# Twelve looked-up tables instead of thirteen, 56 gathers instead of 52, and another place for the last transposes

## What is computed

```python
e = jnp.stack([tbl_0[ids[:, 0]], tbl_1[ids[:, 1]], ..., tbl_25[ids[:, 25]]], axis=1)
all_emb = jnp.concatenate([r_bottom_output[:, None, :], e], axis=1)
z = jnp.einsum('bfd,bgd->bfg', all_emb, all_emb)[:, _TRIU_I, _TRIU_J]
h = jnp.concatenate([z, r_bottom_output], axis=1)
h = jnp.maximum(h @ W_top1 + b_top1, 0.0)
h = jnp.maximum(h @ W_top2 + b_top2, 0.0)
y = h @ W_top3
```

## Time and profile before

| | us |
|---|---|
| median of three runs | 112.02 |
| the three runs | 111.33, 112.02, 112.22 |
| the profiled execution, whole | 113.11 |
| its span in the trace | 111.3 |
| PE busy | 102.7 (92%) |
| PEld busy | 87.2 (78%) |
| DVE busy | 67.5 (61%) |
| ACT busy | 62.0 (56%) |
| POOL busy | 55.9 (50%) |

### The profile page before, as it was taken

One profiled execution on the slowest core, in us unless ns is written; L12 is line 12 of the kernel. 1 busy time (PEld: TensorE's weight loads), 2 busy tenths in 40 slices (PEclk: granted clock), 3 DMA queues, 4 the chain that ended last, 5 costly groups with the idle time before them and its releaser, 6 DMA issues.

```text
span 111.3 us, 3670 instructions
## 1 busy us (share of the span) xinstructions
PE 102.7 (92%) x1562; PEld 87.2 (78%) x1562; DVE 67.5 (61%) x151; ACT 62.0 (56%) x105; POOL 55.9 (50%) x59
## 2 busy tenths in 40 slices
PE   4999999999999999899958999976999989999992
PEld 4767778887888887788947889865999978997970
DVE  3599999999999989999980006400910550082010
ACT  5535996992894899986573124242343246234331
POOL 2777787777777777777777777740000000000000
PEclk9999999999999999999999999999999999999999
DMA  2989999999999999999961212220000000000000
GB/s 73 286 243 233 198 236 211 235 228 221 204 223 236 208 229 231 229 198 226 239 175 47 53 53 53 68 56 0 6 6 0 6 6 0 6 9 0 0 0 0
DMA packets 6369, 13.72 MB, mean 123 GB/s; under 512 B 1984, under 2 KB 2640, under 8 KB 6354
## 3 DMA queue, kind: packets, MB, share of 16 engines
q1 hardware_dynamic: 4520, 10.02, 39.6%
q0 software_dynamic: 1664, 3.41, 13.5%
q10 hardware_dynamic: 170, 0.07, 0.3%
HBM read 13.48 MB, written 0.02 MB: 121 GB/s over the span
## 4 chain that ended last, share of the span: by engine, by line
PE 49%; POOL 24%; issue 12%; DMA 9%; ACT 3%; ACTq 0%
POOL rows L328 24%; PE acc L683 11%; PE acc L649 10%; DMA rows<-tbl,ids_sb 7%; PE ring L693 7%; PE acc L614 6%; PE acc L588 6%; PE acc L674 3%; PE ring L626 3%; PE ring L703 2%; DMA ids_sb<-ids 2%; PE ring L657 1%; ACT emb L400 1%; ACT onehot L389 1%; ACT away L384 0%
## 5 line engine op out<-in xcount | busy, mean ns | idle before, releaser
L328 POOL DMA_INDIRECT rows<-tbl,ids_sb x52 | 55.2, 1061 | 17.2 <-issue 15.5
L498 DVE TENSOR_SCALAR onehot<-far 125x512 fp32r<-125x512 f32 x102 | 38.2, 434 | 1.9 <-ACT far L359 1.9
L588 PE MATMUL acc<-onehot,hi 125*128 125x512 f32 x94 | 26.2, 404 | 0.2 <-DVE onehot L498 0.2
L588 PE MATMUL acc<-onehot,lo 125*128 125x512 f32 x94 | 25.0, 390 | 0.0
L508 DVE COPY gram<-acc 128x432 f32<-128x432 f32 x4 | 3.7, 922 | 29.8 <-PE acc L649 29.8
L588 PEld LDWEIGHTS acc<-onehot,lo 125*128 125x128 f32 x94 | 17.7, 188 | 3.8
L588 PEld LDWEIGHTS acc<-onehot,hi 125*128 125x128 f32 x94 | 16.7, 188 | 4.8 <-DVE onehot L498 1.7
L345 ACT CAST hi<-raw 125x1024 fp32r<-125x1024 f32 (+1 forms) x12 | 13.3, 1105 | 11.3 <-DMA raw<-tbl 6.8
L485 DVE TENSOR_TENSOR lo<-raw,hi 125x512 fp32r<-125x512 f32 (+1 forms) x26 | 18.4, 710 | 0.0
L649 PE MATMUL acc<-emb 128*27 128x27 f32 x1024 | 12.9, 192 | 2.7 <-issue 2.7
L649 PEld LDWEIGHTS acc<-emb 128*27 128x27 f32 x1024 | 10.9, 104 | 5.1 <-issue 3.5
(11 more groups left out here) (41 smaller groups left out, 77.9 us busy)
## 6 DMA issues: line engine op xcount, KB each, us to landing
raw<-tbl SPq DMA_DIRECT2D x9, 448.0 KB
raw<-tbl SPq DMA_DIRECT2D x3, 560.0 KB
ids_b<-ids SPq DMA_DIRECT2D x4, 256.0 KB, 10.6
rows<-tbl,ids_sb POOLq DMA_INDIRECT x52, 8.3
w1z<-w SPq DMA_DIRECT2D x1, 702.0 KB
w_sb<-w SPq DMA_DIRECT2D x1, 512.0 KB
raw<-tbl SPq DMA_DIRECT2D x9, 52.0 KB
raw<-tbl SPq DMA_DIRECT2D x2, 224.0 KB
```

The source lines that it names most:

```text
L328: nc.gpsimd.indirect_dma_start(out=rows[:, t, slot, :], out_offset=None, in_=tables[table], in_offset=bass.IndirectOffsetOnAxis(ap=ids_sb[ ...
L498: ins = nc.vector.tensor_scalar(onehot[:, n % OH_RING, k, :], far[:, t % FAR_RING, :], float(c), None, ALU.is_equal)
L588: mm = nc.tensor.matmul(acc[:, look_bank(t), :], part_of[:, t % HL_RING, c * D:(c + 1) * D], onehot[:, n % OH_RING, k, :], start=(half == ...
```

## The change

Table 13 is no longer looked up but gathered. That leaves 12 looked-up tables (table 12 moves behind table 18) and 14 gathered ones, in four groups a tile of 4, 4, 4 and 2. Pairs are now (0,1), (2,3), up to (10,11), and the last table's chunks are all compared by VectorE. Turn (2,0) no longer stands behind a look; the turns of tile 2 follow later in the second part of the order, and turns (3,2) and (3,3) stand ahead of `bottom` (2,1).

```diff
-LOOKED_UP = [1, 2, 4, 8, 16, 17, 12, 18, 20, 13, 21, 24, 25]
-LONG = [8, 12, 13]
+LOOKED_UP = [1, 2, 4, 8, 16, 17, 18, 12, 20, 21, 24, 25]
+LONG = [8, 12]
...
-    behind = {2: (0, 0), 3: (0, 1), 4: (0, 2), 5: (0, 3), 6: (1, 0), 7: (1, 1), 8: (1, 2), 9: (1, 3), 10: (2, 0)}
+    behind = {2: (0, 0), 3: (0, 1), 4: (0, 2), 5: (0, 3), 6: (1, 0), 7: (1, 1), 8: (1, 2), 9: (1, 3)}
...
-              ("turn", 2, 1),
+              ("turn", 2, 0),
...
-              ("gram", 0, 2), ("part", NL - 1, 2), ("turn", 2, 2), ("gram", 0, 3), ("part", NL - 1, 3),
-              ("turn", 2, 3), ("bottom", 0, 0), ("bottom", 0, 1), ("gram", 1, 0), ("turn", 3, 0), ("bottom", 1, 0),
+              ("gram", 0, 2), ("part", NL - 1, 2), ("turn", 2, 1), ("gram", 0, 3), ("part", NL - 1, 3),
+              ("bottom", 0, 0), ("bottom", 0, 1), ("turn", 2, 2), ("gram", 1, 0), ("bottom", 1, 0),
...
 def paired(j):
 
-    return j > 0 and (NL - 1 - j) % 2 == 0
+    return j % 2 == 1
 
 
 def by_act(j):
 
-    return LOOKED_UP[j] in LONG or paired(j)
+    return LOOKED_UP[j] in LONG or paired(j) and j < NL - 1
...
-        idb_in = [sem(f"idb_in{k}") for k in range((NL - FIRST + 1) // 2)]
+        idb_in = [sem(f"idb_in{k}") for k in range((NL - FIRST) // 2)]
...
-                    n = 2 if paired(t) else 1
-                    if paired(t) or t == 0:
-                        first, b = slot_of(t - n + 1), look_bank(t - n + 1)
+                    if paired(t):
+                        first, b = slot_of(t - 1), look_bank(t - 1)
...
-                        pe.wait_ge(emb_look, t - LOOK + (1 if paired(t - LOOK) or t == LOOK else 2))
+                        pe.wait_ge(emb_look, (t - LOOK) // 2 * 2 + 2)
```

More of the change, by code:

```diff
@@ L107, in work_order @@
     order += [("compare", NL - 1, 0), ("part", NL - 2, 0), ("part", NL - 2, 1), ("part", NL - 1, 0), ("part", NL - 1, 1),
-              ("turn", 2, 1),
+              ("turn", 2, 0),
               ("gram", 0, 0), ("part", NL - 2, 2), ("gram", 0, 1), ("part", NL - 2, 3),
-              ("gram", 0, 2), ("part", NL - 1, 2), ("turn", 2, 2), ("gram", 0, 3), ("part", NL - 1, 3),
-              ("turn", 2, 3), ("bottom", 0, 0), ("bottom", 0, 1), ("gram", 1, 0), ("turn", 3, 0), ("bottom", 1, 0),
[L112 to L116, removed]
+              ("gram", 0, 2), ("part", NL - 1, 2), ("turn", 2, 1), ("gram", 0, 3), ("part", NL - 1, 3),
+              ("bottom", 0, 0), ("bottom", 0, 1), ("turn", 2, 2), ("gram", 1, 0), ("bottom", 1, 0),
+              ("gram", 1, 1), ("pairs", 0, 0), ("turn", 2, 3), ("gram", 1, 2), ("l1", 0, 0), ("l1", 0, 1), ("gram", 1, 3),
+              ("l1", 0, 2), ("l1", 0, 3), ("turn", 3, 0), ("bottom", 1, 1),
+              ("gram", 2, 0), ("l2", 0, 0), ("gram", 2, 1), ("l2", 0, 1), ("pairs", 1, 0), ("bottom", 2, 0), ("turn", 3, 1),
+              ("gram", 2, 2), ("l1", 1, 0), ("l1", 1, 1), ("gram", 2, 3), ("l1", 1, 2), ("l1", 1, 3), ("turn", 3, 2),
+              ("turn", 3, 3), ("bottom", 2, 1),
               ("gram", 3, 0), ("l2", 1, 0), ("gram", 3, 1), ("pairs", 2, 0), ("l2", 1, 1), ("l3", 0, 0),
@@ L279, in load_ids @@
             def load_ids(k):
[L280 to L283, removed]
+                sp.dma_start(ids_b[:, 2 * k:2 * k + 2, :].rearrange("p j b -> p (j b)"),
+                             ids_16[FIRST + 2 * k:FIRST + 2 * k + 2, :].rearrange("j b -> (j b)").unsqueeze(0)
+                             .broadcast_to([128, 2 * B])).then_inc(idb_in[k], 16)
             sp.dma_start(idt_i[:], ids_t).then_inc(idt_in, 16)
@@ L395, in _ @@
                         split(t + HL_RING)
-                    n = 2 if paired(t) else 1
-                    if paired(t) or t == 0:
-                        first, b = slot_of(t - n + 1), look_bank(t - n + 1)
+                    if paired(t):
+                        first, b = slot_of(t - 1), look_bank(t - 1)
                         act.wait_ge(oh_used, 2 * (t + 1))
-                        nc.scalar.copy(emb[:, :, :, first:first + n],
-                                       acc[:, b:b + n, :].rearrange("d j (t p) -> d t p j", t=TILES)
-                                       ).then_inc(emb_look, n)
+                        nc.scalar.copy(emb[:, :, :, first:first + 2],
+                                       acc[:, b:b + 2, :].rearrange("d j (t p) -> d t p j", t=TILES)
+                                       ).then_inc(emb_look, 2)
                     if t == NL // 2:
```

## The result

| | before, us | changed, us | ratio, 95% interval |
|---|---|---|---|
| first series | 112.02 | 109.19 | 0.9723 (0.968 to 0.9767) |
| second series, another chip | 112.69 | 108.95 | 0.9697 (0.9637 to 0.9756) |

The forecast was 108.9, a ratio of 0.972, within 107.2 to 110.6. The kernel became about 3% faster. Times are medians of all executions, ratios go by the fast ones alone, and the profiled execution of the first series was a slow one (112.3 us, with TensorE's granted clock at 0.50 from 48.3 to 51.7), so the profile read here is that of the second series: 108.96 us, span 107.0, granted clock 1.0 in every slice. The trace of the kernel before was taken with the first series, so the two traces compared are of different series.

What follows compares the result with a forecast made beforehand. The looks were held by TensorE, VectorE, DMA engines and gather issue together, the second part by TensorE. Terms -4.0 (looks), +0.5 (transposes) and +0.4 (stops) sum to -3.1 us: 112.02 becomes 108.9, range 107.2 to 110.6.

Steps and rivals of the forecast that it cites:

- What bounds: Looks: TensorE, VectorE and DMA engines nearly equally full, with gathers at their own pace; from gram (0,0) on, TensorE.
- milestone 1: Start of turn (1,2) in the looks: gather 26 lands at 46.7, start at 46.8, 1.8 us later; TensorE idles about 2.
- Milestone 2: Turn (1,2) to first gram: onehot wait goes, last cast is late next; parts end at 55.5, 4.0 us earlier.
- The last turns: Turn (3,3) ahead of the bottom product: gains nothing beyond 0.11 to 0.2; tile 3's gram 1.7 us after turn (3,2).
- The second part: From gram (0,0) to the end, bound by TensorE: +0.5 us for transposes and +0.4 for stops.
- the transposes: Behind gram (0,0): 24 instead of 18, +0.66 with some given back, net +0.5 us (bounds 0.2 and 1.2).
- TensorE's stops: Inside grams, at boundaries 127 or 128 matmuls apart that shift by 21: +0.4 us (bounds -1.0 and +1.5).
- the gathers land in time: Rival at turn (1,2): gather 26 lands before 44.7, parts end 1.4 to 2.0 earlier, time 107.3 us; chance 0.15.
- The worse join: Rival at the last table's parts: late gather 32, cast or compares, parts take 5.8 us, time 111.0; chance 0.12.
- Late last gathers: Rival at turn (3,3): gather 56 lands late, at 88.8 taking back 2.8 us, at 91.8 giving 114.7; chance 0.04.

Runs made afterwards that it cites:

- f1_act_last: Changed kernel with the last table's chunk 0 made by ScalarE again, on a third chip: 110.75 us, ratio 0.9826.
- c2_turn_late: Changed kernel with turn (1,2) one look later, behind look 9, and turn (1,3) behind the parts: 107.97 us, ratio 0.9607.
- a4_act_last: Changed kernel with the last table's chunk 0 made by ScalarE again, on a slow chip: 158.75 us against 162.03 for the kernel before.
- e1_act_last: Changed kernel with the last table's chunk 0 made by ScalarE again, on a second slow chip: 162.25 us against 164.33 for the kernel before.
- c1_again: Changed kernel once more, unchanged, on another chip (the second series): 108.95 us, ratio 0.9697.
- a2_turn_late: Changed kernel with turn (1,2) behind look 9 and turn (1,3) behind the parts, on a slow chip: 160.47 us against 162.03 for the kernel before.
- a3_fill: Changed kernel with 8 identity matmuls (16 records) ahead of turn (1,2)'s wait, on a slow chip: 160.39 us against 162.03 for the kernel before.
- a1_again: Changed kernel once more, unchanged, on a slow chip: 159.73 us against 162.03 for the kernel before.

## Why the prediction was right, and where not

**What bounds, and milestone 1: right.** The prediction said that gather 26, not the freed TensorE, sets turn (1,2): landing at 46.7, start at 46.8. It landed at 47.1, because it was issued at 38.70 instead of 38.16 (the 8.44 us to landing were as forecast), and the turn started at 47.28, against 44.98 before. The wait was put at 2 us and was 1.70, in the traces of the first series and of f1_act_last 2.26 and 2.46, with the turn at 47.53 and 47.47 (from 47.5 on the prediction had called itself wrong, so the first series' trace is just past that); c2_turn_late, where that wait is gone and the parts end 1.91 earlier, shows that it was on the path. What I left out is turn (1,1), which waited 1.11 for gather 22 in the same way. As far as three traces show, it cost nothing of its own: turn (1,1) waited 1.11, 0.69 and 0.33, turn (1,2) waited the longer the less turn (1,1) had, and the two together make 2.8 to 3.0 in each.

**Milestone 2: right.** From turn (1,2) to the end of the parts 8.7 us were forecast (4.1 and 4.6) and 8.79 measured (4.12 to the end of look 9, 4.67 behind it), then 0.92 as forecast. The wait for ScalarE's onehot went and the cast became what is late next, 1.38 us of waiting on VectorE and 0.24 on TensorE. f1_act_last, a4_act_last and e1_act_last show the first half of that by bringing the wait back. The looks gained 3.47 us in the trace, instead of 4.0.

**The last turns: right.** Turn (3,3) ahead of the bottom product bought nothing: tile 3's gram came 1.71 after turn (3,2), against 1.69, and 0.44 of it is still idle. No turn of tiles 2 and 3 waited for its rows. That this order is worth nothing was read from the one trace and not tried by itself.

**The second part: its term was too high, and the stops were mis-sized.** The terms were +0.5 for the transposes and +0.4 for TensorE's stops, +0.9 together; from gram (0,0) to the end it was 50.0 us instead of 50.8, so -0.8. One pair of traces doesn't settle the sign: the thirteen traces of the changed kernel and its variants took 49.3 to 51.5 there, 50.0 in the mean, and of the kernel before there is only the one. But all thirteen lie under the 51.7 that the forecast amounts to. The transposes are there (24 behind gram (0,0)), and cost what they cost: turn (3,2) and (3,3) together 0.66. It is the term of the stops that was mis-sized. A gram step without a stop takes 0.67 us from its start to the next instruction's. What the twelve steps of tiles 0 to 2 took above that, stops and smaller stretches together, was 2.7 us before and 1.6 in c1_again, 2.7 in the first series, 2.3 in c2_turn_late and 1.4 in f1_act_last: between -1.4 and 0.0 where +0.4 was forecast. Before, the two long stops were 0.80 and 1.01. In c1_again there is one:

```profile
69.03 0.41 PE L647 MATMUL acc<-emb 128*27 128x27 f32 x29
70.21 0.46 PE L647 MATMUL acc<-emb 128*27 128x27 f32 x35 [0.78 <-issue]
```

In the profiled execution of the first series, at full clock from 52 us on, there are three:

```profile
60.63 0.32 PE L647 MATMUL acc<-emb 128*27 128x27 f32 x17
61.38 0.59 PE L647 MATMUL acc<-emb 128*27 128x27 f32 x47 [0.44 <-issue]
...
71.90 0.41 PE L647 MATMUL acc<-emb 128*27 128x27 f32 x29
73.27 0.46 PE L647 MATMUL acc<-emb 128*27 128x27 f32 x35 [0.96 <-issue]
...
80.27 0.62 PE L647 MATMUL acc<-emb 128*27 128x27 f32 x51
81.19 0.30 PE L647 MATMUL acc<-emb 128*27 128x27 f32 x13 [0.30 <-issue]
```

The places were right. Between these three stops lie 381 and 254 matmuls, which is 3 and 2 times the 127 of before. They stand where the prediction put them, one in the parts between the first grams, one in gram (1,2) and one in tile 2's gram. The middle one came behind 7 matmuls before and behind 29 after, where 21 fewer records ahead of it give 28. In c2_turn_late it is behind 29 as well, for 0.80, and in f1_act_last too, for 0.52, though there these grams ran 1.2 us earlier and 1.4 later. That gram (1,3), which stopped for 1.01 before, would run through in c1_again was right as well.

The sizes were not. At the same place in the program a stop costs something else in each execution: in gram (1,2) 0.41 to 0.98 over the thirteen traces, in gram (0,1) nearly nothing in c1_again (0.70 us for 0.67), 0.44 in the first series and 0.42 in a2_turn_late, in gram (2,1) 0.24 in c1_again, 0.30 in the first series and nothing in f1_act_last. A fixed least time for 128 records, worked out from a single pair of stops, was too strict.

The Trainium skill (Runtime: NRT & Kernel Launch, Instruction fetch mechanics) has blocks of 256 instructions, which agrees with the 127 pairs between the stops and with a stop that moves as the program ahead of it shrinks or grows. It has the crossing "mostly hidden"; here the stop in gram (1,2), if it is such a crossing, showed in every trace, by 0.41 to 0.98 us, while gram (1,3) and gram (0,2) of c1_again ran through in 0.67. The profile's page lists 12 instruction transfers of 0.20 MB in all. That such a transfer is what TensorE stops for was not shown by itself.

**The rest** is in the end: 0.3 us less from tile 3's gram on, where nothing was changed. Sum of the terms in the traces: -3.5 in the looks and -0.8 behind them, 4.3 us of span. The profiled execution of before was 1.1 us over its median, which can explain why the medians show less, 2.8 and 3.7. That these lie around the forecast 3.1 is in part luck: in this pair of traces the looks gained 0.5 less than forecast and the second part came out 1.7 better.

**The rivals.** That the gathers land in time did not happen, though most of them came sooner than before: those issued from 42 to 46 took 7.5, against 8.4 to 8.6, but number 26 took 8.44. By the Trainium skill (DMA: Bandwidth & Descriptors, Anatomy of one DMA) an estimate would be 2.2; the late ones now take 2.5, the ones beside table loads do not. The worse join did not come either: the cast was late, but VectorE had 1.80 us of idling to spare, and the join took 4.67 us and not 5.8. Late last gathers were not seen: no turn of tile 3 waited.

## What to carry to other kernels

When work moves from a busy engine to a stream of transfers that is issued at a fixed rate, count which transfer each consumer now waits for: here the last gather of each of tile 1's first three groups moved one place back, that of tile 3's last group four, and the first freed microseconds went into waiting for it. Then move the consumer, not the transfer; a turn one look later took the wait away and showed the next bound, which was VectorE. And after each such gain expect the next engine within a microsecond or two where two engines are busy for 96% and more of the time and the DMA engines are full, as here. A term smaller than what traces of nearly the same program differ by (here 2.2 us in the second part) can't be confirmed from one trace of each.

## What the runs showed of the hardware that was not expected

TensorE's stops inside runs of equal matmuls keep their place in the program from trace to trace, 127 matmuls or a multiple apart, and move by as many records as are taken out or put in ahead of them, within one: 22 places for 21 taken out, 15 for 16 put in. Their length does not keep, 0.41 to 0.98 us at one and the same place.

In the first series' trace TensorE had idled 2.26 us before turn (1,2); its granted clock was full until 48.3, then 0.50 until 51.7, and look 9 took 5.34 us instead of 3.74. In f1_act_last it idled 2.46 us at the same place, and the clock stayed full. So the idling alone does not decide it, and why the clock fell is open. (The 0.6 to 0.7 in the expectation of a3_fill are means of slices of 2.8 us.)

On the chips of the first series, of c1_again and of f1_act_last the kernel before took 112 to 113 us; on three others the same program took 162 to 164. The changed kernel's trace there (a1_again) has TensorE, VectorE and ScalarE idle for much of the looks until the last gather was issued. Why a chip does this is open. A gain measured on such a chip says nothing about the looks; what stands behind the last gather can be read there.
